# A selective scan with routed ternary experts: u\*B of 14 turns made by ScalarE and turned back by TensorE, products in place, ring of six

## The chip, the cores and the metric

One Trainium2 chip, one core. The time is the device time of one execution in microseconds (us), on the one core that runs. The engines work side by side, each with its own program in order, and meet in semaphores: TensorE (PE, with its weight loads PEld), VectorE (DVE), ScalarE (ACT), GpSimd (POOL), and SyncE (SP), which here only issues transfers.

## What is computed

Two layers on x of shape (2, 1024, 256). The scan is where the change lies; the second layer (each token goes through the weights of one of 32 masked experts) is untouched, except that its masks are brought in during the scan.

```
A = -exp(A_log);  x_dbl = x @ W_xproj.T;  delta, Bmat, Cmat = split(x_dbl, (64, 16, 16))
delta = softplus(delta @ W_dt.T + b_dt)
deltaA = exp(delta[..., None] * A)
BX = delta[..., None] * Bmat[:, :, None, :] * x[..., None]
for each time step:  h = dA * h + bx;  y = einsum('bdn,bn->bd', h, c)
y = y + D * x
```

u below is delta\*x, so that BX is u\*B.

## The kernel before, in words

Channels lie on the 128 partitions and time (L = 1024) along the free axis. There are 2 batches x 2 halves of the 256 channels = 4 groups, and 16 states n in each: 64 turns, k = 16 group + n. A turn k is:
- the decay exp(delta\*A) of 128x1024, made by ScalarE (`decay`, L562) one turn ahead
- u\*B of 128x1024. In 44 turns TensorE spreads the row of B over the partitions into PSUM (`b_rows`, L1011, two matmuls) and VectorE multiplies it by u in place (`scan`, L783). In 20 turns (states 2, 5, 8, 11, 14) SyncE brings the row of B from memory (`load_b`), and GpSimd multiplies (`bx`, L392); there ScalarE writes the decay into the PSUM buffer that no b row needs
- the scan over time on VectorE (L788), which writes h into one of four buffers
- h\*C on GpSimd (`product`, L400) into one of four more, with the row of C brought by SyncE (`load_c`)
- the sum over n on TensorE (`sums`, L1046: two matmuls with the identity, each run as two), three turns later. In states 4 to 11 `skip_and_residual` (L1035, L1037) adds D\*x and x.

The order of each engine is written out by hand in loops over k. On TensorE iteration k is: the b row of k+1 (after scan k-1), the sums of k-3, skip and residual, `prepare`, then one mask's four transposes (L1027, turns 20 to 51). `prepare` makes z of a half of delta (`delta_in`, L977; k = 1, 4, 11, 13, 15, 17) and the projection for batch 1 (`project`, L971; k = 7, 9). On ScalarE iteration k is: decay k+1, the copy of a finished delta (L513), the copy of the mask's transposes out of PSUM (`mask_out`, L550), then the soft part (`soft_part`, four ACTIVATE of 512 columns, L502 to L507) or the projection's copy (`low_out`, L491) of that iteration. All of these go through one PSUM bank, `w_ps`. VectorE finishes delta and u (`delta_u`, L756 and L758) after turns 2, 5, 12, 14, 16, 18, and converts the projection to bf16 parts after turns 8, 10, 11, 13 (L744, L748), with GpSimd in between.

The tile `xs_sb` holds h and the products in this phase, `xn` holds b rows for GpSimd, `rows` holds delta and u, `cst` the identity, `mask_sb` the masks and, late in the scan, b rows too (`b_buffer`).

## Time and profile before

| | us |
|---|---|
| median of 3 runs | 345.85 (345.0 to 347.11) |
| the profiled execution | 345.58 |
| its span in the trace | 343.7 |
| VectorE busy in the span | 297.3 (86%) |
| GpSimd busy | 271.7 (79%) |
| TensorE busy (matmul) | 251.1 (73%) |
| ScalarE busy | 159.3 (46%) |
| turns 0 to 15, start to start | 31.06 to 89.65 |
| turns 16 to 31 | 89.65 to 141.82 |
| turns 32 to 47 | 141.82 to 190.72 |
| turns 48 to 63, with the last product | 190.72 to 244.28 |

The page and the trace come from one execution, taken by the hardware profiler. A row of the timeline gives the start, the length, the engine, the line, the operation with out<-in and the count of instructions merged in it; the bracket behind it, where there is one, is the time the engine stood idle before it and who released it. PEclk is the granted clock of TensorE as a share of its full 2.4 GHz. A length is longer than the distance to the next start where neighbours overlap.

### The profile page before, as it was taken

What the parts mean: (1) busy time and instruction counts of PE and PEld (TensorE: products, weight loads), DVE (VectorE), ACT (ScalarE), POOL (GpSimd) and SP (SyncE); (2) the same over time, 40 slices, a digit from 0 to 9 for tenths busy, and PEclk for the clock granted to TensorE, in tenths of its full rate; (3) what the DMA queues carried; (4) which work ended last, traced back from release to release, by engine and by line L of the source; (5) the groups of instructions that cost most, each with busy time, mean ns of one, the idle gap of its engine ahead of it and who ended that gap; (6) DMA issues with size and microseconds to landing.
All of it is one profiled execution on the core that took longest, in us unless ns stands there. A gap on an engine that the chain in (4) does not pass through costs nothing.

```text
span 343.7 us, 3843 instructions
## 1 busy us (share of the span) xinstructions
PE 251.1 (73%) x1183; PEld 144.1 (42%) x1184; DVE 297.3 (86%) x369; ACT 159.3 (46%) x216; POOL 271.7 (79%) x153
## 2 busy tenths in 40 slices
PE   0676498994968998979899798797970006999740
PEld 0422144441324654435565344453550003899640
DVE  1999999999999999999999997999989896656650
ACT  1375755447468565556445743333265501444210
POOL 0473988999888999999999959999937770377772
PEclk9995599997889999989999989898995555999885
DMA  7425799999998799988999773762001557898400
GB/s 243 132 75 185 251 297 300 359 376 317 315 373 273 265 331 311 301 307 296 330 314 317 259 237 106 259 219 97 2 1 52 196 212 260 286 291 270 155 2 0
DMA packets 36355, 78.80 MB, mean 229 GB/s; under 512 B 5027, under 2 KB 15789, under 8 KB 36336
## 3 DMA queue, kind: packets, MB, share of 16 engines
q1 hardware_dynamic: 23744, 63.15, 55.9%
q10 hardware_dynamic: 9776, 9.09, 8.2%
q0 software_dynamic: 2816, 6.32, 4.9%
q8 instruction: 10, 0.16, 0.2%
q14 instruction: 9, 0.07, 0.1%
HBM read 63.55 MB, written 17.09 MB: 235 GB/s over the span
## 4 chain that ended last, share of the span: by engine, by line
DVE 41%; PE 20%; issue 15%; DMA 9%; POOL 7%; ACT 6%; ACTq 0%; another core or an unknown queue 0%; SPq 0%; POOLq 0%; DVEq 0%
DVE xs_sb L788 16%; PE bank L1046 11%; DVE bank L783 9%; DMA xs_sb<-sorted_tokens 4%; PE bank L1011 2%; PE bank L1198 2%; POOL out_dram L457 2%; DMA x_sb<-in_L_attn_x_dram 2%; DMA out_dram<-cb,to_token 2%; POOL sorted_tokens L447 2%; ACT dA L562 2%; DVE st L817 2%; POOL xs_sb L400 1%; DVE xn L717 1%; POOL mask_sb L392 1%
## 5 line engine op out<-in xcount | busy, mean ns | idle before, releaser
L400 POOL TENSOR_TENSOR xs_sb<-xs_sb,cb 128x1024 f32<-128x1024 f32 x63 | 147.6, 2363 | 8.0 <-DVE xs_sb L788 5.3
L1046 PE MATMUL bank<-xs_sb,cst 128*128 128x512 f32 x256 | 130.8, 639 | 1.1 <-ACT xn L567 1.1
L788 DVE TENSOR_TENSOR_SCAN xs_sb<-dA,bank 128x1024 f32<-128x1024 f32 x44 | 100.6, 2286 | 1.5
L1046 PEld LDWEIGHTS bank<-xs_sb,cst 128*128 128x128 f32 x256 | 51.0, 205 | 47.5 <-issue 38.4
L783 DVE TENSOR_TENSOR bank<-bank,rows 128x1024 f32<-128x1024 f32 x44 | 53.3, 1210 | 0.1
L1011 PE MATMUL bank<-bc,pick 96*128 96x512 bf16 x88 | 30.3, 433 | 31.0 <-DVE xs_sb L788 31.0
L562 ACT ACTIVATE dA<-rows,a_neg 128x1024 f32<-128x1024 f32 x44 | 49.5, 1139 | 0.9 <-DVE rows L756 0.5
L457 POOL DMA_INDIRECT out_dram<-cb,to_token x32 | 31.8, 993 | 22.2 <-DVE cb L934 15.4
L392 POOL TENSOR_TENSOR xn<-xn,rows 128x1024 f32<-128x1024 f32 x16 | 37.6, 2352 | 5.4 <-DMA xn<-bc_rows 5.2
L788 DVE TENSOR_TENSOR_SCAN xs_sb<-bank,xn 128x1024 f32<-128x1024 f32 x16 | 36.3, 2271 | 0.3 <-ACT bank L562 0.2
L562 ACT ACTIVATE bank<-rows,a_neg 128x1024 f32<-128x1024 f32 x20 | 22.3, 1114 | 27.5 <-DVE xs_sb L788 27.5
L550 ACT ACTIVATE wT<-bank 128x512 f16<-128x512 bf16 x32 | 19.1, 597 | 34.3 <-PE bank L1027 33.9
L671 ACT ACTIVATE xn<-bank 128x1024 f16<-128x1024 f16 x16 | 16.3, 1024 | 38.4 <-PE bank L1181 38.4
L1198 PE MATMUL bank<-wT,xn 128*128 x256 | 32.3, 283 | 0.4 <-ACT xn L671 0.4
L1198 PEld LDWEIGHTS bank<-wT,xn 128*128 128x128 f16 x256 | 25.3, 101 | 4.2 <-issue 0.9
L1011 PEld LDWEIGHTS bank<-bc,pick 96*128 96x128 bf16 x88 | 6.8, 106 | 43.6 <-DVE xs_sb L788 39.7
L447 POOL DMA_INDIRECT sorted_tokens<-rows,pos x16 | 15.8, 986 | 4.9 <-issue 4.3
L1035 PEld LDWEIGHTS bank<-xnT,diag_d 128*128 128x128 f32 x64 | 12.2, 191 | 15.6 <-issue 15.6
L926 DVE TENSOR_TENSOR cb<-bank,scale_bc 128x512 f32<-128x512 f32 x16 | 11.0, 687 | 7.7 <-PE bank L1198 7.7
L934 DVE SCALAR_TENSOR_TENSOR cb<-cb,xs_sb 128x256 f32<-128x256 f32 x32 | 14.2, 483 | 2.0 <-DVE to_token L929 0.5
L1027 PEld LDWEIGHTS bank<-ident_bf,mask_sb 128*128 128x128 bf16 x128 | 10.1, 105 | 7.9 <-issue 7.7
L1163 PE MATMUL bank<-cst,cb 64*1 64x64 f32 x2 | 0.4, 285 | 17.5 <-DVE cb L906 17.5
(142 smaller groups left out, 335.7 us busy)
## 6 DMA issues: line engine op xcount, KB each, us to landing
cb<-bc_rows SPq DMA_DIRECT2D x63, 512.0 KB, 5.4
sorted_tokens<-wT SPq DMA_DIRECT2D x32, 257.0 KB, 10.7
xn<-bc_rows SPq DMA_DIRECT2D x16, 512.0 KB, 6.7
mask_sb<-_L_ffn_expert_masks_dram ACTq DMA_DIRECT2D x32, 256.0 KB, 5.8
xs_sb<-sorted_tokens SPq DMA_DIRECT2D x7, 1028.0 KB, 8.2
x_sb<-in_L_attn_x_dram SPq DMA_DIRECT2D x4, 512.0 KB, 7.7
mask_sb<-bc_rows SPq DMA_DIRECT2D x4, 512.0 KB, 5.7
xs_sb<-sorted_tokens SPq DMA_DIRECT2D x2, 514.0 KB, 4.3
```

Of the source, the lines that this page charges most:

```text
L392: pool.tensor_tensor(b_buffer(k), b_buffer(k), u[:, dh, b * L:(b + 1) * L], ALU.mult).then_inc(s_gbx, 1)
L400: pool.tensor_tensor(prod[:, j, :], h[:, j, :], cb[:, j, :], ALU.mult).then_inc(s_prod, 1)
L447: pool.indirect_dma_start(xs, bass.IndirectOffsetOnAxis(ap=pos[:, t:t + 1], axis=0), rows[:, t, :], None).then_inc(s_scat, 16)
L457: pool.indirect_dma_start(out_v, bass.IndirectOffsetOnAxis(ap=to_token[:, 2 * f + blk:2 * f + blk + 1], axis=0), y_sb[:, f, blk, :], None, ...
L550: act.activation(wT[:, e, :, :].rearrange("p h o -> p (h o)"), mask_ps, ACT.Copy).then_inc(s_wt, 1)
L562: act.activation(to, delta[:, dh, b * L:(b + 1) * L], ACT.Exp, scale=a_neg[:, dh, n:n + 1]).then_inc(s_da, 1)
L671: act.activation(xsT_tiles[:, j, :, 0::2, :], bank[:, j, :].bitcast(fp16).rearrange("p (a s t) -> p a s t", s=2, t=M), ACT.Copy).then_inc( ...
L783: dve.tensor_tensor(bx, bx, u[:, dh, b * L:(b + 1) * L], ALU.mult).then_inc(s_bx, 1)
L788: dve.tensor_tensor_scan(h[:, j, :], decays, bx, 0.0, ALU.mult, ALU.add).then_inc(s_scan, 1)
L1011: mm = pe.matmul(b_ps[k % 2][:, c * HC:(c + 1) * HC], pick[:, n:n + 1].to_broadcast([96, P]), bc3[:, cols], start=True, stop=True)
L1046: mm = pe.matmul(yacc[:, c * HC:(c + 1) * HC], ident, prod[:, j, c * HC:(c + 1) * HC], start=first, stop=last, skip_group_check=True)
L1198: mm = pe.matmul(bank[:, 2 + f, blk * D:(blk + 1) * D], xsT[:, f % 2, blk, part, odd * M:odd * M + P], wT[:, bass.ds(experts[tile], 1), pa ...
```

## The change

- ScalarE makes u\*B of 14 turns (states 6, 8, 10, 12, 14 of group 0, states 3, 7, 11 of the others), two turns ahead. Since B varies along time and u along channels and time, it works on u with time on the partitions: TensorE turns u of the group (`turn_u`, in eight pieces over iterations 2, 3, 12, 14, 19, 20, 44, 45) and B (`turn_b`, iterations 0 and 10), ScalarE copies both out (`u_T_out`, `b_T_out`), and `act_bx` multiplies eight blocks of 128x128 by a column of B each. TensorE turns the eight blocks back into the PSUM buffer in which a b row would stand (`turn_bx`); VectorE scans from there without a multiply.
- GpSimd has 16 turns instead of 20 (states 1, 5, 9, 13), VectorE 34 instead of 44.
- A mask leaves PSUM one iteration later on ScalarE (k - 1 in place of k).
- h\*C is written over h, and the ring of h is six buffers deep: the scan of k waits for the sum of k-6, no more for the product of k-4. The room left holds u\*B turned and a b row of its own.
- The b row of the first GpSimd turn is asked for ahead of the second c row.

```diff
-POOL_STATES = (2, 5, 8, 11, 14)
+HELD = 6
+POOL_STATES = (1, 5, 9, 13)
+ACT_STATES = ((6, 8, 10, 12, 14), (3, 7, 11), (3, 7, 11), (3, 7, 11))
...
+        BT_AT = {0: 0, 10: 1}
+        UT_AT = {2: (0, 0), 3: (0, 1), 12: (1, 0), 14: (1, 1), 19: (2, 0), 20: (2, 1), 44: (3, 0), 45: (3, 1)}
...
-                if k >= masks_done:
-                    sp.wait_ge(s_mps, E - 2 + 2 * (i % 2))
+                if in_masks(i):
+                    sp.wait_ge(s_mps, E - 2)
...
-                pool.tensor_tensor(prod[:, j, :], h[:, j, :], cb[:, j, :], ALU.mult).then_inc(s_prod, 1)
+                here = h[:, k % HELD, :]
+                pool.tensor_tensor(here, here, cb[:, j, :], ALU.mult).then_inc(s_prod, 1)
...
+            def act_bx(k):
+                i, g, n = of_act[k], k // N, k % N
+                act.wait_ge(s_utsb, LH * (g + 1))
+                act.wait_ge(s_btsb, g // DH + 1)
+                if i >= 1:
+                    act.wait_ge(s_bready, of_psum[act_turns[i - 1]] + 1)
+                for c in range(LB):
+                    ins = act.activation(u_b_T[:, c, :], u_T(g)[:, c, :], ACT.Copy,
+                                         scale=b_T[:, g // DH * LB + c, n:n + 1])
+                ins.then_inc(s_abx, 1)
...
-                if 0 <= k - MASK_FROM < E:
-                    mask_out(k - MASK_FROM)
+                if 0 <= k - 1 - MASK_FROM < E:
+                    mask_out(k - 1 - MASK_FROM)
+                if k in BT_AT:
+                    b_T_out(BT_AT[k])
+                if k in UT_AT:
+                    u_T_out(*UT_AT[k])
+                if k + 2 in act_turns:
+                    act_bx(k + 2)
                 if k in SOFT_AT:
                     soft_part(SOFT_AT[k], w_ps)
...
-                if k >= RING:
-                    dve.wait_ge(s_prod, k - 3)
-                dve.tensor_tensor_scan(h[:, j, :], decays, bx, 0.0, ALU.mult, ALU.add).then_inc(s_scan, 1)
+                if k >= HELD:
+                    dve.wait_ge(s_sum, k - HELD + 1)
+                dve.tensor_tensor_scan(h[:, k % HELD, :], decays, bx, 0.0, ALU.mult, ALU.add).then_inc(s_scan, 1)
...
+            def turn_bx(k):
+                i = of_act[k]
+                pe.wait_ge(s_abx, i + 1)
+                pe.wait_ge(s_scan, k - 1)
+                for c in range(LB):
+                    mm = pe.transpose(b_ps[k % 2][:, c * P:(c + 1) * P], u_b_T[:, c, :], ident)
+                mm.then_inc(s_bready, 1)
...
-                if k + 1 < TURNS and k + 1 not in pool_turns:
+                if k + 1 in act_turns:
+                    turn_bx(k + 1)
+                elif k + 1 < TURNS and k + 1 not in pool_turns:
                     b_rows(k + 1)
```

ScalarE before, from decay 6 to the copy of the second projection (iterations 5 to 9 of group 0; L491 is that copy, and what it waits for is in the bracket):

```order
L562 ACTIVATE dA<-rows,a_neg 128x1024 [waits scan_done] x2
L513 ACTIVATE rows<-bank 128x512 [waits u_ready]
L562 ACTIVATE bank<-rows,a_neg 128x1024 [waits scan_done]
L491 ACTIVATE xd<-bank 96x512 [waits bc3_ready,bc_rows_written,z_ready,projected]
L562 ACTIVATE dA<-rows,a_neg 128x1024 [waits scan_done]
L540 DMA mask_sb<-in_L_ffn_expert_masks_dram 128x2x256 x4
L562 ACTIVATE dA<-rows,a_neg 128x1024 [waits scan_done]
L491 ACTIVATE xd<-bank 96x512 [waits bc3_ready,bc_rows_written,z_ready,projected]
```

The same stretch of ScalarE in the changed kernel (L585 is the decay, L603 `act_bx`, L512 the projection's copy):

```order
L585 ACTIVATE dA<-rows,a_neg 128x1024 [waits scan_done] x2
L534 ACTIVATE rows<-bank 128x512 [waits u_ready]
L603 ACTIVATE xs_sb<-xn,b_T 128x128 [waits b_ready,b_transposed_evacuated,u_transposed_evacuated]
L603 ACTIVATE xs_sb<-xn,b_T 128x128 x7
L585 ACTIVATE dA<-rows,a_neg 128x1024 [waits scan_done]
L512 ACTIVATE xd<-bank 96x512 [waits bc3_ready,bc_rows_written,z_ready,projected]
L585 ACTIVATE bank<-rows,a_neg 128x1024 [waits scan_done]
L561 DMA mask_sb<-in_L_ffn_expert_masks_dram 128x2x256 x4
L603 ACTIVATE xs_sb<-xn,b_T 128x128 [waits b_ready,b_transposed_evacuated,u_transposed_evacuated]
L603 ACTIVATE xs_sb<-xn,b_T 128x128 x7
L585 ACTIVATE dA<-rows,a_neg 128x1024 [waits scan_done]
L512 ACTIVATE xd<-bank 96x512 [waits bc3_ready,bc_rows_written,z_ready,projected]
```

Two blocks of eight pieces have come in, each a decay ahead of a copy that waits for TensorE's projection.

TensorE before, iterations 7 and 8 and the start of 9 (L1046 sums, L1035 and L1037 skip and residual, L971 the projection, L1011 a b row):

```order
L1046 MATMUL bank<-xs_sb,cst 128x512 [waits product_ready]
L1046 MATMUL bank<-xs_sb,cst 128x512
L1035 MATMUL bank<-xnT,diag_d 128x128
L1037 MATMUL bank<-cst,x_sb 128x128
L971 MATMUL bank<-xnT,wxT 96x512 [waits xnT_ready,xd_ready,abs_ready]
L971 MATMUL bank<-xnT,wxT 96x512
L1011 MATMUL bank<-bc,pick 128x512 [waits scan_done]
```

TensorE in the changed kernel, the same iterations (L1093 is `turn_bx`, L1127 the sums, L1116 and L1118 skip and residual, L1020 the projection):

```order
L1093 MATMUL bank<-cst,xs_sb 128x128 [waits scan_done,transposed_bx_ready]
L1093 MATMUL bank<-cst,xs_sb 128x128 x7
L1127 MATMUL bank<-xs_sb,cst 128x512 [waits product_ready]
L1127 MATMUL bank<-xs_sb,cst 128x512
L1116 MATMUL bank<-xnT,diag_d 128x128
L1118 MATMUL bank<-cst,x_sb 128x128
L1020 MATMUL bank<-xnT,wxT 96x512 [waits xd_ready,xnT_ready,u_transposed_evacuated,abs_ready]
L1020 MATMUL bank<-xnT,wxT 96x512
L1127 MATMUL bank<-xs_sb,cst 128x512 [waits product_ready]
L1127 MATMUL bank<-xs_sb,cst 128x512
L1116 MATMUL bank<-xnT,diag_d 128x128
L1118 MATMUL bank<-cst,x_sb 128x128
```

Iteration 7, which began with the sums, now begins with eight transposes that wait for ScalarE's u\*B of turn 8, and the projection stands behind them. The before list has the b row of turn 9 (its turn 9 was VectorE's, now it is GpSimd's).

## Rows read from the trace of the kernel before

**Rows 1.** Busy us and instructions per engine in two stretches, clock, DMA share, GB/s

```profile
48.40:89.70 41.30, 34.80 (x101) 16.16 (x101) 40.71 (x30) 21.33 (x27) 37.91 (x18) 0.92 1.05 345
141.80:190.70 48.90, 45.01 (x214) 25.61 (x214) 48.52 (x28) 26.84 (x33) 48.64 (x21) 0.97 0.90 308
```

**Rows 2.** Timeline of VectorE, group 2: start, us, engine, line, operation

```profile
145.27 1.21 DVE L783 TENSOR_TENSOR bank<-bank,rows 128x1024 f32<-128x1024 f32 x1
146.51 2.29 DVE L788 TENSOR_TENSOR_SCAN xs_sb<-dA,bank 128x1024 f32<-128x1024 f32 x1
148.71 2.27 DVE L788 TENSOR_TENSOR_SCAN xs_sb<-bank,xn 128x1024 f32<-128x1024 f32 x1
150.90 1.21 DVE L783 TENSOR_TENSOR bank<-bank,rows 128x1024 f32<-128x1024 f32 x1
```

**Rows 3.** Timeline of GpSimd, group 2: three products, then one u\*B

```profile
146.67 6.96 POOL L400 TENSOR_TENSOR xs_sb<-xs_sb,cb 128x1024 f32<-128x1024 f32 x3
153.59 2.35 POOL L392 TENSOR_TENSOR xn<-xn,rows 128x1024 f32<-128x1024 f32 x1
```

**Rows 4.** Waits from 60 to 236 us: total us, times, longest

```profile
DVE xs_sb L788 <- POOL mask_sb L392: 2.7, 2, 2.0
```

**Rows 5.** Timeline of ScalarE: two 128-column casts, four 256-column pieces

```profile
235.79 0.29 ACT L610 ACTIVATE ident<-cst 128x128 f16<-128x128 f32 x1
235.99 0.29 ACT L611 ACTIVATE tri_bf<-cst 128x128 bf16<-128x128 f32 x1
...
254.18 2.06 ACT L620 ACTIVATE xn<-rows,shift,rstd 128x256 f32<-128x256 f32 x4
```

**Rows 6.** Timeline of TensorE: four transposes to a mask, one whole iteration to the next

```profile
120.80 0.60 PE L1018 MATMUL bank<-cst,w_nat 128*128 128x128 f32 x4
121.24 0.39 PE L1027 MATMUL bank<-ident_bf,mask_sb 128*128 128x128 bf16 x4
...
157.98 0.60 PE L1011 MATMUL bank<-bc,pick 96*128 96x512 bf16 x2
158.41 1.88 PE L1046 MATMUL bank<-xs_sb,cst 128*128 128x512 f32 x4
160.13 0.38 PE L1035 MATMUL bank<-xnT,diag_d 128*128 128x128 f32 x2
...
160.80 0.38 PE L1011 MATMUL bank<-bc,pick 96*128 96x512 bf16 x1
```

**Rows 7.** Timeline of ScalarE, group 0: a soft part to the next decays, decay 5

```profile
35.70 0.67 ACT L502 ACTIVATE wT<-bank,bdt 128x512 f32<-128x512 f32 x1
...
38.18 2.17 ACT L562 ACTIVATE dA<-rows,a_neg 128x1024 f32<-128x1024 f32 x2
...
45.05 1.12 ACT L562 ACTIVATE bank<-rows,a_neg 128x1024 f32<-128x1024 f32 x1 [2.86 <-DVE xs_sb L788]
...
59.88 1.15 ACT L562 ACTIVATE dA<-rows,a_neg 128x1024 f32<-128x1024 f32 x1 [0.45 <-issue]
```

**Rows 8.** Timeline of VectorE, group 0: delta and u to the next multiply; turn 16

```profile
50.55 0.67 DVE L756 SCALAR_TENSOR_TENSOR bank<-wT,bank 128x512 f32<-128x512 f32 x1
...
51.87 1.22 DVE L783 TENSOR_TENSOR bank<-bank,rows 128x1024 f32<-128x1024 f32 x1
...
89.65 1.21 DVE L783 TENSOR_TENSOR bank<-bank,rows 128x1024 f32<-128x1024 f32 x1
```

**Rows 9.** Timeline of TensorE behind two idle times

```profile
148.86 0.60 PE L1011 MATMUL bank<-bc,pick 96*128 96x512 bf16 x2 [2.35 <-DVE xs_sb L788]
149.30 3.08 PE L1046 MATMUL bank<-xs_sb,cst 128*128 128x512 f32 x4
...
218.03 1.00 PE L1011 MATMUL bank<-bc,pick 96*128 96x512 bf16 x2 [1.96 <-DVE xs_sb L788]
218.83 3.22 PE L1046 MATMUL bank<-xs_sb,cst 128*128 128x512 f32 x4
```

**Rows 10.** Window behind the first of them, columns as in Rows 1

```profile
150.00:153.00 3.00, 3.00 (x8) 1.07 (x7) 2.96 (x3) 0.58 (x1) 3.00 (x2) 0.50 0.68 264
```

More of the change, by code:

```diff
@@ L105, in selective_scan_then_routed_ternary_ffn @@
         flat = "p a l -> p (a l)"
-        before = prod[:, :, :].rearrange(flat)
+        before = h_and_prod[:, 4 * L:8 * L]
         wx_nat = before[0:96, 1024:1024 + D]
@@ L199, in selective_scan_then_routed_ternary_ffn @@
         s_bload = [sem(f"b_loaded{j}") for j in range(2)]
+        s_btps = sem("b_transposed")
+        s_btsb = sem("b_transposed_evacuated")
+        s_utps = sem("u_transposed")
+        s_utsb = sem("u_transposed_evacuated")
+        s_abx = sem("transposed_bx_ready")
         s_gbx = sem("bx_ready_from_gpsimd")
@@ L986, in _, with turned_b, turned_u @@
                 delta_in(m, bank[:, m, :])
+            def turned_b(k):
+                return sum(1 for at in BT_AT if at < k)
+            def turned_u(k):
+                return sum(1 for at in UT_AT if at < k)
             def prepare(k):
@@ L1085, in _ @@
                 if k >= LAG:
-                    sums(k - LAG, (k - LAG) % RING, first=(n == LAG), last=(n == LAG - 1))
+                    sums(k - LAG, (k - LAG) % HELD, first=(n == LAG), last=(n == LAG - 1))
                 if RING <= n < RING + LB:
@@ L1091, in _ @@
                 prepare(k)
+                if k in BT_AT:
+                    pe.wait_ge(s_xnsb, 2 * DH * LH)
+                    if k:
+                        pe.wait_ge(s_low, B * LH)
+                    turn_b(BT_AT[k])
+                if k in UT_AT:
+                    pe.wait_ge(s_btsb, turned_b(k))
+                    if turned_u(k):
+                        pe.wait_ge(s_utsb, turned_u(k))
+                    pe.wait_ge(s_abs, 2 + sum(1 for at in SOFT_AT if at < k))
+                    if k > MASK_FROM:
+                        pe.wait_ge(s_wt, k - MASK_FROM)
+                    turn_u(*UT_AT[k])
                 if k == ROUTER_AT:
@@ L1129, in turn_x1 @@
                 mm.then_inc(s_yps, 1)
-            sums(TURNS - 3, (TURNS - 3) % RING)
+            sums(TURNS - 3, (TURNS - 3) % HELD)
             pe.wait_ge(s_scan, TURNS)
@@ L1137, in _ @@
             turn_x1(3)
-            sums(TURNS - 2, (TURNS - 2) % RING)
-            sums(TURNS - 1, (TURNS - 1) % RING, last=True, apart=True)
+            sums(TURNS - 2, (TURNS - 2) % HELD)
+            sums(TURNS - 1, (TURNS - 1) % HELD, last=True, apart=True)
             for c in range(LH):
```

75 lines of the change are left out of this document (54 added, 21 removed).

## The prediction

> **What bounds the kernel now.** I read the busy times by stretch first, then the timeline of VectorE, then those of the others around it, and last the waits. In the windows [rows 1], turns 32 to 47 (the third group, 48.9 us) have VectorE busy for 48.5 us and GpSimd for 48.6: two engines are full at once. TensorE is busy 45.0, and ScalarE only 26.8. In turns 5 to 15 of group 0 (41.3 us) VectorE is busy 40.7, GpSimd 37.9, ScalarE 21.3. So VectorE sets the pace throughout, GpSimd beside it from group 1 on.
>
> The timeline of VectorE gives the price of a turn from start to start [rows 2]: multiply to scan 145.27 to 146.51 = 1.24, scan to next 146.51 to 148.71 = 2.20, so 3.44 for a turn whose u\*B it makes (M turn) and 2.2 for a turn whose u\*B GpSimd makes (148.71 to 150.90). GpSimd's pieces cost (153.59 - 146.67) / 3 = 2.31 each [rows 3]. Sixteen turns cost VectorE 11 x 3.44 + 5 x 2.2 = 48.8, GpSimd 21 x 2.31 = 48.5. One more wait stands on this path: GpSimd's b row for a buffer in the mask tile comes late, and VectorE loses 2.7 us in group 3 [rows 4].
>
> **What the change takes away.** VectorE multiplies in 34 turns instead of 44: 10 x 1.24 = 12.4 us, of which 4 x 1.24 = 5.0 fall in group 0 and 2 x 1.24 in each later group (7.4). GpSimd loses 4 u\*B, 9.2 us; a group of it is then 20 x 2.31 = 46.2, VectorE's 9 x 3.44 + 7 x 2.2 = 46.4. Both go down together, so groups 1 to 3 can return 7.4 us. The b row of turn 53 is asked for three turns ahead of GpSimd's use now and only two loads go to the mask tile: I take the 2.7 us as returned as well. Four loads of 512 KB fewer, and one moved ahead of the second c row, touch nothing that waits. Product in place and the ring of six cost nothing: scan k now waits for sum k-6, which TensorE does three turns ahead. Masks out a turn late spare ScalarE waits that cost nothing, since it is half idle [rows 1].
>
> **What it adds, in the later groups.** On ScalarE a turn of its own costs eight pieces of 128 columns. The nearest rows are the plain 128-column casts, 0.20 from start to start (below), and 256-column pieces with two pointer operands, (2.06 - 0.59) / 3 = 0.49 (above) [rows 5]. The decays show what one pointer adds, some 0.09: 0.29 a piece, and 2.4 us for the eight with the last one's tail. Both ends: 1.7 and 4.0. On TensorE a turn adds eight transposes; four of the same shape take 121.24 - 120.80 = 0.44, so 0.88, in place of a b row's 0.43 [rows 6]. An iteration of TensorE with b row, sums, skip and mask takes 160.80 - 157.98 = 2.82, of which 0.43 for the row, 1.72 for the sums, 0.67 for the rest. Four turns (two with b rows, one GpSimd's, one ScalarE's) are then 2.82 + 2.39 + 2.82 + 3.27 = 11.3 against VectorE's 2 x 3.44 + 2 x 2.2 = 11.3 and GpSimd's 5 x 2.31 = 11.55. That is tight only where skip and masks meet (four such quads, one of them with logits, 0.9 more). In the others TensorE has 1.8 us of slack. I charge 3.0 us of new stalls there: 0.9 for the logits quad, some 0.3 for each other tight quad, and 1 at turns 18 to 22, where ScalarE has its last soft parts, the first y copy and the bf16 moves in a row.
>
> The Trainium skill ("ScalarE: Activation LUTs", Rules for kernel authors) budgets about 0.3 us for each ACTIVATE plus 0.83 ns an element. By that the eight would be 3.2 us, and the sum below 5 x 0.85 = 4 us longer. The casts' 0.20 from start to start speaks against it, as do their durations of 0.29, all of it included.
>
> **What it adds in group 0: the step that decides.** There ScalarE also has the soft parts, (38.18 - 35.70) = 2.5 us each, and its decays, 1.06 [rows 7]. Above all the program order now ties two engines to each other. ScalarE makes u\*B of turn k+2, then must wait for TensorE's projection or z of its next iteration; but TensorE's iteration starts with the turning back of just that u\*B, ahead of sums, skip and projection. In the kernel before, those iterations (7, 9, 11, 13) started with a b row, or with nothing, and asked ScalarE for neither. I walk it from decay 5, which starts at 45.05 now [rows 7] and, as ScalarE has copies of u and B out ahead of it, at about 45.5 after:
> - ScalarE: decay 1.06, u\*B of 6 2.4, soft part 2.5, decays 6 and 7 2.1, a copy 0.55, u\*B of 8 2.4: 11.0 (56.6)
> - TensorE, iteration 7: 0.1 + 0.88 + 1.72 + 0.44 + projection 1.72 + tail 0.16 = 5.0 (61.6)
> - ScalarE: copy 0.6, decay 1.06, issue of four mask loads 0.45 [rows 7], u\*B of 10 2.4: 4.5 (66.1)
> - TensorE, iteration 9, the same 5.0, and iteration 10 (row 0.43, sums 1.72, skip 0.44, turning B 0.88): 3.5 (74.6)
> - ScalarE: B out 0.3, u\*B of 12 2.4: 2.7 (77.3)
> - TensorE, iteration 11: 0.1 + 0.88 + 1.72 + 0.44 + z 0.86 + 0.16 = 4.2 (81.5)
> - ScalarE: soft part 2.5, decay 1.06, u out 0.55, u\*B of 14 2.4: 6.5 (88.0)
> - TensorE, iteration 13, no skip: 3.7 (91.7)
> - ScalarE soft part 2.5, then VectorE delta and u (51.87 - 50.55 = 1.32 [rows 8]) and turn 15 at 3.44: 7.3 (99.0).
>
> Turn 16 starts at 99.0 instead of 89.65 [rows 8]: **+9.3 us**, although VectorE has 5.0 less to do. VectorE stands still in between (the scans of 10 and 12, the conversions after 8 and 10, deltas 4 and 5), and nothing covers it: GpSimd waits for the same scans.
>
> On top, TensorE is idle in this walk for 2.5 us before iteration 9, 2.8 before 11 and 4.4 before 13. After an idle time of 2.35 us and one of 1.96 us the profile shows the granted clock at 0.50, of its two levels 1.2 GHz, and four sums take over 3 us [rows 9, 10]; a stretch of 3 us at that level costs 1.5 to 1.7. Before, that cost nothing; now these iterations are on the path. Three times 1.6: **+4.8**.
>
> **Sum**, against the profiled execution of 345.58 (span 343.7), which is within 0.3 us of the median 345.85: +9.3 + 4.8 - 7.4 - 2.7 + 3.0 = +7.0, so 352.6 us.
>
> **Rivals.**
> - *The clock stays up, or the pieces are cheap.* Idle times of just over 2 us might miss a fall. For: at 148.86 the row itself was still fast. Without the 4.8 the time is 347.8; with pieces at 0.20 as well (5 x 0.7 less) about 344. Chance 0.26, nearly all of it within 1%.
> - *The pieces are dear*, as two pointers' 0.49 would have them: 1.6 more for each of five in group 0 (+8), and in the tight quads of the later groups TensorE waits for them: about 362. With the 0.3 us and 0.83 ns of the Trainium skill ("ScalarE: Activation LUTs", Rules) it would be 357. The copy with one pointer is nearer to a plain cast. Chance 0.15.
> - *TensorE becomes the bound in the later groups*: 11.3 us of work in 11.3, so each fall of the clock and each late piece stays. Some four losses of 1.6: 359. Against: outside skip and mask turns it has slack to catch up. Chance 0.10.
> - *Faster: ScalarE and TensorE do not hold each other in group 0.* ScalarE's own work for turns 5 to 16 is 12 decays, 5 u\*B, 4 soft parts, 8 copies: 39.4 us, so it would be through by 85, and turn 16 could start near 87, 2.6 earlier than now. With 7.4 and 2.7 returned and 1 of stalls, 334. It decides from the point where its waits for TensorE in group 0, 15 us in the walk, fall under some 3. For: VectorE alone needs less. Against: the order of the two programs, and waits of the same kind are there already. Chance 0.08.
>
> The forecast itself has 0.41. Range 344.5 to 359: from the cheap end of the first rival to the third. A measurement of this kernel tells about 1% from no change, 342.4 and 349.3. Slower 0.41 + 0.15 + 0.10 = 0.66; faster 0.09 (the last rival and the edge of the first); the same 0.25.
>
> **What would show it.** In the new timeline turn 16's multiply starts at 97 to 105 us; ScalarE waits for TensorE before the two projections' copies and soft parts 4 and 5 by 2 to 4 us each; TensorE waits for ScalarE's u\*B before iterations 9, 11 and 13, with the granted clock at 0.50 behind it; the pieces start 0.29 apart; groups 2 and 3 take 46.4 to 48 us each, and the 2.7 us at the mask buffer are gone. I am wrong if turn 16 starts before 93, or if groups 1 to 3 give back less than 7 us in all, for then a bound that I hold for slack has moved in.

## The result and the profile after

The changed kernel takes 353.91 us (median of 4 executions, 352.4 to 355.75) against 346.48 for the kernel before on the same chip: ratio 1.0225, 95% interval 1.0182 to 1.0268. It is slower by 2.2%; the whole interval lies above 1. The forecast was 352.6 with a range of 344.5 to 359. The profiled execution is the one of 352.4 us (span 350.6), so it is 6.9 us of span longer than the one of before. Two of the traces read below, of the kernels called "projection and z first" and "the same, u\*B before mask", come from slow executions, 1.6% above the fastest of their kernel, which the ratios leave out.

Reading the time by stretch, from the window view: start and end, length, busy us and instructions of TensorE, its weight loads, VectorE, ScalarE and GpSimd, then granted clock, DMA share, GB/s. The four stretches are turns 5 to 15, and groups 1, 2 and 3 up to VectorE's last product.

```profile
47.80:100.50 52.70, 40.84 (x155) 21.45 (x154) 34.25 (x25) 34.49 (x70) 37.88 (x18) 0.97 1.01 306
100.50:153.50 53.00, 45.04 (x213) 25.64 (x213) 49.15 (x30) 39.84 (x70) 45.23 (x20) 1.00 0.77 240
153.50:204.70 51.20, 45.88 (x232) 27.36 (x231) 46.62 (x26) 34.64 (x59) 46.83 (x21) 0.97 0.85 286
204.70:251.80 47.10, 43.42 (x184) 24.54 (x183) 46.16 (x26) 27.18 (x48) 45.74 (x21) 1.00 0.53 190
```

Against [rows 1]: in turns 5 to 15 VectorE's work fell from 40.7 us to 34.3, but the stretch grew from 41.3 to 52.7, so VectorE, which was full, now stands still a third of the time, and GpSimd's 37.9 are the same work spread wider. In group 2 VectorE's work fell by 1.9 and the stretch grew by 2.3; no engine fills it now. Only in group 3 does the length follow VectorE's work again.

The same in positions (start of a turn's first VectorE instruction, us):

| turn | before | after | shift | gained or lost since the turn above |
|---|---|---|---|---|
| 16 | 89.65 | 100.53 | +10.9 | +10.9 |
| 32 | 141.82 | 153.54 | +11.7 | +0.8 |
| 48 | 190.72 | 204.72 | +14.0 | +2.3 |
| last product | 243.00 | 251.85 | +8.9 | -5.2 |
| end of span | 343.7 | 350.6 | +6.9 | -1.9 |

Where VectorE stands still in group 0, from its timeline (start, us, line, operation; in brackets the idle time ahead of it and what ended it). The row of turn 16 is the last; before, it stood in [rows 8].

```profile
67.00 2.29 DVE L838 TENSOR_TENSOR_SCAN xs_sb<-dA,bank 128x1024 f32<-128x1024 f32 x1 [1.91 <-PE bank L1093]
71.50 0.56 DVE L793 CAST bc<-xd 32x512 bf16<-32x512 f32 x1 [2.21 <-ACT xd L512]
77.88 2.29 DVE L838 TENSOR_TENSOR_SCAN xs_sb<-dA,bank 128x1024 f32<-128x1024 f32 x1 [1.78 <-PE bank L1093]
83.69 0.70 DVE L805 SCALAR_TENSOR_TENSOR bank<-wT,bank 128x512 f32<-128x512 f32 x1 [3.52 <-ACT bank L528]
...
95.74 0.69 DVE L805 SCALAR_TENSOR_TENSOR bank<-wT,bank 128x512 f32<-128x512 f32 x1 [4.73 <-ACT bank L528]
...
100.53 1.21 DVE L833 TENSOR_TENSOR bank<-bank,rows 128x1024 f32<-128x1024 f32 x1
```

L1093 is TensorE turning u\*B back, L512 ScalarE's copy of the projection, L528 the last step of a soft part. The releasers alternate between TensorE and ScalarE, as two engines that hold each other would show. Their own timelines have the other half: ScalarE (first fence) waits for TensorE's projection (L1020) and z (L1026), TensorE (second fence) for ScalarE's u\*B (L603).

```profile
61.11 0.59 ACT L512 ACTIVATE xd<-bank 96x512 f32<-96x512 f32 x1 [4.02 <-PE bank L1020]
...
74.09 0.28 ACT L589 ACTIVATE b_T<-bank 128x128 f32<-128x128 f32 x1 [1.58 <-PE bank L1077]
74.26 2.43 ACT L603 ACTIVATE xs_sb<-xn,b_T 128x128 f32<-128x128 f32 x8
...
81.09 0.69 ACT L523 ACTIVATE wT<-bank,bdt 128x512 f32<-128x512 f32 x1 [3.36 <-PE bank L1026]
...
93.14 0.69 ACT L523 ACTIVATE wT<-bank,bdt 128x512 f32<-128x512 f32 x1 [4.08 <-PE bank L1026]
```

```profile
65.87 1.09 PE L1093 MATMUL bank<-cst,xs_sb 128*128 128x128 f32 x8 [2.63 <-ACT xs_sb L603]
66.80 1.88 PE L1127 MATMUL bank<-xs_sb,cst 128*128 128x512 f32 x4
...
76.75 1.09 PE L1093 MATMUL bank<-cst,xs_sb 128*128 128x128 f32 x8 [2.69 <-ACT xs_sb L603]
77.68 1.88 PE L1127 MATMUL bank<-xs_sb,cst 128*128 128x512 f32 x4
...
87.59 1.10 PE L1093 MATMUL bank<-cst,xs_sb 128*128 128x128 f32 x8 [4.18 <-ACT xs_sb L603]
88.52 3.38 PE L1127 MATMUL bank<-xs_sb,cst 128*128 128x512 f32 x4
```

The four sums take 1.88 us behind idle times of 2.63 and 2.69, and 3.38 behind that of 4.18. The windows (length, busy TensorE, granted clock, DMA share, GB/s) show why: the clock fell to 0.50, its lower level of 1.2 GHz, once in this stretch, and TensorE's idle time of 4.18 us ends just ahead of it.

```profile
76.00:78.00 2.00, 1.25 (x9) 1.00 0.91 311
...
88.00:90.00 2.00, 2.00 (x10) 0.69 1.04 304
90.00:92.00 2.00, 2.00 (x4) 0.50 0.97 220
```

And VectorE's waits from turn 16 on (total us, times, longest); of [rows 4] nothing is left.

```profile
DVE bank L833 <- PE bank L1070: 5.8, 6, 1.6
DVE xs_sb L838 <- ACT dA L585: 1.0, 1, 1.0
DVE xs_sb L838 <- ACT bank L585: 0.8, 1, 0.8
DVE xs_sb L838 <- PE bank L1093: 0.5, 1, 0.5
```

They are 8.1 us in nine places: 0.77, 1.63 and 0.96 before turns 21, 24 and 27 (3.4 in group 1); 1.58, 0.38, 0.54, 0.90 and 0.75 before turns 36, 40, 43, 44 and 46 (4.2 in group 2); 0.58 before turn 52.

### The profile page after: what moved, and what is told of

Same layout as the page of the kernel before. It is cut to its first block, busy times and chain, and to the rows that moved or that the text cites. A ratio compares the mean times of both kernels' runs of the same rounds, so it can differ in the third digit from the quotient of the medians.

```text
span 350.6 us, 4272 instructions
## 1 busy us (share of the span) xinstructions
PE 255.9 (73%) x1324; PEld 153.9 (44%) x1324; DVE 282.2 (80%) x359; ACT 194.8 (56%) x338; POOL 263.6 (75%) x149
## 4 chain that ended last, share of the span: by engine, by line
PE 27%; DVE 23%; ACT 17%; issue 16%; DMA 8%; POOL 6%; ACTq 1%; SPq 0%; POOLq 0%; DVEq 0%
PE bank L1127 13%; ACT xs_sb L603 7%; DVE xs_sb L838 5%; DVE bank L833 5%; POOL out_dram L478 4%; DMA out_dram<-cb,to_token 4%; PE bank L1093 3%; DMA x_sb<-in_L_attn_x_dram 2%; POOL sorted_tokens L468 2%; PE bank L1070 2%; PE bank L1020 2%; DVE st L866 1%; ACT dA L585 1%; PE bank L1108 1%; PE bank L1012 1%
## 5 line engine op out<-in xcount | busy, mean ns | idle before, releaser
L1127 PE MATMUL bank<-xs_sb,cst 128*128 128x512 f32 x256 | 125.6, 615 | 1.1 <-ACT xn L610 1.1
L838 DVE TENSOR_TENSOR_SCAN xs_sb<-dA,bank 128x1024 f32<-128x1024 f32 x48 | 109.1, 2283 | 7.3 <-PE bank L1093 5.2
L1127 PEld LDWEIGHTS bank<-xs_sb,cst 128*128 128x128 f32 x256 | 47.6, 196 | 41.3 <-issue 35.0
L585 ACT ACTIVATE dA<-rows,a_neg 128x1024 f32<-128x1024 f32 x48 | 54.3, 1139 | 0.6 <-DVE rows L805 0.5
L833 DVE TENSOR_TENSOR bank<-bank,rows 128x1024 f32<-128x1024 f32 x34 | 41.3, 1216 | 6.1 <-PE bank L1070 5.8
L603 ACT ACTIVATE xs_sb<-xn,b_T 128x128 f32<-128x128 f32 x112 | 34.1, 389 | 0.7 <-issue 0.7
L1070 PE MATMUL bank<-bc,pick 96*128 96x512 bf16 x68 | 22.6, 416 | 9.1 <-DVE xs_sb L838 9.0
L1093 PE MATMUL bank<-cst,xs_sb 128*128 128x128 f32 x112 | 15.2, 279 | 15.3 <-ACT xs_sb L603 15.3
L585 ACT ACTIVATE bank<-rows,a_neg 128x1024 f32<-128x1024 f32 x16 | 17.8, 1114 | 10.8 <-DVE xs_sb L838 10.8
L413 POOL TENSOR_TENSOR xs_sb<-xs_sb,rows 128x1024 f32<-128x1024 f32 x8 | 18.8, 2355 | 3.3 <-DVE rows L807 3.3
L1093 PEld LDWEIGHTS bank<-cst,xs_sb 128*128 128x128 f32 x112 | 12.1, 142 | 18.5 <-ACT xs_sb L603 18.5
L1116 PEld LDWEIGHTS bank<-xnT,diag_d 128*128 128x128 f32 x64 | 12.2, 190 | 15.3 <-issue 15.3
L838 DVE TENSOR_TENSOR_SCAN xs_sb<-bank,xs_sb 128x1024 f32<-128x1024 f32 x8 | 18.2, 2270 | 0.6 <-PE bank L1127 0.6
L1108 PE MATMUL bank<-ident_bf,mask_sb 128*128 128x128 bf16 x128 | 12.4, 220 | 6.1 <-ACT wT L571 4.2
```

Source lines behind the costliest of these rows:

```text
L585: act.activation(to, delta[:, dh, b * L:(b + 1) * L], ACT.Exp, scale=a_neg[:, dh, n:n + 1]).then_inc(s_da, 1)
L603: ins = act.activation(u_b_T[:, c, :], u_T(g)[:, c, :], ACT.Copy, scale=b_T[:, g // DH * LB + c, n:n + 1])
L833: dve.tensor_tensor(bx, bx, u[:, dh, b * L:(b + 1) * L], ALU.mult).then_inc(s_bx, 1)
L838: dve.tensor_tensor_scan(h[:, k % HELD, :], decays, bx, 0.0, ALU.mult, ALU.add).then_inc(s_scan, 1)
L1070: mm = pe.matmul(b_ps[k % 2][:, c * HC:(c + 1) * HC], pick[:, n:n + 1].to_broadcast([96, P]), bc3[:, cols], start=True, stop=True)
L1093: mm = pe.transpose(b_ps[k % 2][:, c * P:(c + 1) * P], u_b_T[:, c, :], ident)
```

## The experiments

The experiments ran on four chips. On two of them the kernel before takes 346 us, on the others 357 and 358; each ratio is to the kernel before on the same chip in the same batch. Positions inside the loop do not depend on the chip (below), so they are compared across all of them. The table gives the starts of turns 16, 32 and 48 and the end of the last scan.

| kernel | turn 16 | turn 32 | turn 48 | last scan ends | ratio to before, 95% |
|---|---|---|---|---|---|
| before | 89.65 | 141.82 | 190.72 | 242.9 | 1 |
| after | 100.53 | 153.54 | 204.72 | 251.8 | 1.0225 (1.0182 to 1.0268) |
| after, again | 102.56 | 155.57 | 206.77 | 253.8 | 1.0219 (1.0172 to 1.0266) |
| no u\*B in group 0 | 91.17 | 145.14 | 194.69 | 241.7 | 0.9957 (0.9906 to 1.0008) |
| projection and z first | 92.38 | 145.41 | 194.97 | 242.0 | 0.9889 (0.9846 to 0.9932) |
| one piece | 95.82 | 148.13 | 196.39 | 242.8 | 0.9975 (0.9939 to 1.0011) |
| masks in time | 102.59 | 166.86 | 230.35 | 279.1 | 1.0998 (1.0930 to 1.1066) |
| before, masks late | 88.82 | 140.29 | 189.09 | 240.9 | 0.9997 (0.9963 to 1.0030) |
| no u\*B on ScalarE | 90.81 | 144.71 | 194.78 | 244.9 | 1.0024 (0.9997 to 1.0052) |
| mask before y | 101.41 | 155.38 | 203.81 | 250.5 | one execution, 355.22 to 346.07 |
| no skip (no u\*B in group 0) | 90.57 | 143.00 | 191.43 | 238.5 | one execution, 339.61 to 346.07 |
| TensorE filled | 99.54 | 153.56 | 204.78 | 251.8 | 1.0204 (1.0149 to 1.0259) |
| first and four | 89.10 | 142.89 | 191.31 | 237.7 | 0.9860 (0.9823 to 0.9897) |
| the same, u\*B before mask | 91.75 | 144.19 | 193.16 | 241.3 | 0.9844 (0.9772 to 0.9915) |

**The theory** is the prediction's: group 0 is lost because the order of two programs ties ScalarE and TensorE to each other. Its rivals: ScalarE's own work is too much there (the pieces), or the falls of the clock are what costs.

### Group 0: without its u\*B on ScalarE

```diff
-ACT_STATES = ((6, 8, 10, 12, 14), (3, 7, 11), (3, 7, 11), (3, 7, 11))
+ACT_STATES = ((), (3, 7, 11), (3, 7, 11), (3, 7, 11))
```

> The changed kernel with no ScalarE turn in group 0 (its five are VectorE's again; u of group 0 is still turned). Theory A, the order ties ScalarE and TensorE together in group 0: VectorE's own work sets group 0 (12 x 3.44 + 4 x 2.2 + 9.2 for deltas and conversions = 59.3 us from 30.3), turn 16 starts at 90 to 91 instead of 100.5, and the time falls by some 10 us to 344. Theory B, the loss lies in what group 0 does for the turned copies of u and B and in the in-place ring: turn 16 stays above 97 and the time above 351.

Turn 16 starts at 91.17, 9.4 earlier, and all of it reaches the end of the loop (241.7 against 251.8). The part for group 0 alone costs the changed kernel its whole loss; the ratio, 0.9957 (0.9906 to 1.0008), cannot be told from that of the kernel before. Of the 1.5 us by which turn 16 still lies behind [rows 8], 1.2 are one multiply more in this stretch: GpSimd made u\*B of turns 8, 11 and 14 there, and makes that of 9 and 13 now.

ScalarE waits for TensorE here as long as in the changed kernel: for the two projections, z and the turned B 18.4 us from 48 us to turn 16, against 17.3 there. Those waits cost nothing as long as TensorE does not wait for ScalarE in turn. In this kernel it does not in that stretch; in the changed one it waits five times (total us, times, longest):

```profile
PE bank L1093 <- ACT xs_sb L603: 11.9, 5, 4.2
```

### Group 0: the same work in another order

```diff
+                if k in PROJECT_AT or (k in SOFT_AT and k > 1):
+                    prepare(k)
                 if k + 1 in act_turns:
                     turn_bx(k + 1)
...
-                prepare(k)
+                if k == 1:
+                    prepare(k)
```

> The changed kernel, but TensorE's projection or z of an iteration stands ahead of the transposes that wait for ScalarE's u*B. Nothing else moves. Theory A (the order ties the two engines): the waits of ScalarE for the projections and soft parts 4 and 5 (15.6 us in the profile after) fall under 7, turn 16 starts at 91 to 95, and the time is 345 to 349. Theory C (ScalarE's own work is too much in group 0, 12 decays, 40 pieces and 4 soft parts): turn 16 stays at 98 to 101, since those are as long as before, and the time moves by less than 2 us.

Nothing is taken away here, ScalarE has all five turns; only TensorE makes projection and z ahead of the turning back. Turn 16 starts at 92.38, 8.15 earlier, and the time falls below that of the kernel before. ScalarE's waits for the projections and for z, 15.5 us in the changed kernel, are gone; it waits 8.4 us for the turned B and u instead. VectorE's waits up to turn 16 were 18.1 us in nine places (nearly all of the difference between its 34.3 us of work and 52.7); three are left, one of 1.22 at 51.66 and these:

```profile
84.72 2.29 DVE L838 TENSOR_TENSOR_SCAN xs_sb<-dA,bank 128x1024 f32<-128x1024 f32 x1 [3.40 <-PE bank L1093]
...
92.38 1.23 DVE L833 TENSOR_TENSOR bank<-bank,rows 128x1024 f32<-128x1024 f32 x1 [0.60 <-PE bank L1070]
```

That separates the theory from the first rival: the amount of work is the same and the time is gone, so it was the order. The gain in time is larger than the trace shows: by the ratio the kernel is 1.1% (4 us) faster than the one before, and in the trace the last scan ends only 0.9 us earlier (242.0 against 242.9). Where the rest lies is open.

### Group 0: cheaper pieces

```diff
-                for c in range(LB):
-                    ins = act.activation(u_b_T[:, c, :], u_T(g)[:, c, :], ACT.Copy,
-                                         scale=b_T[:, g // DH * LB + c, n:n + 1])
+                ins = act.activation(u_b_T[:, :, :], u_T(g)[:, :, :], ACT.Copy,
+                                     scale=b_T[:, g // DH * LB, n:n + 1])
```

> The changed kernel, but ScalarE makes u*B turned in one ACTIVATE of 1024 columns with one column of B for all eight blocks, so that the values of h in 14 turns are others than the reference's; the transposes stay. It costs 1.14 instead of 2.43 us. Theory A: each of the five in group 0 is on the path, 5 x 1.3 = 6.5, turn 16 starts near 94, and the time is 346 to 348.5. Theory D (TensorE alone holds VectorE there, ScalarE's pieces are covered): less than 2 us of it is seen.

The line groups of ScalarE (count | busy, mean ns) give the price of both, the changed kernel in the first fence:

```profile
L603 ACT ACTIVATE xs_sb<-xn,b_T 128x128 f32<-128x128 f32 x112 | 34.1, 389 | 0.7 <-issue 0.7
```

```profile
L602 ACT ACTIVATE xs_sb<-xn,b_T 128x1024 f32<-128x1024 f32 x14 | 15.9, 1139 | 0.7 <-issue 0.7
```

Eight pieces take 2.43 from first to last, one takes 1.14: 1.29 less a turn. Turn 16 starts at 95.82, 4.7 earlier, which is 3.6 of the five savings: most of them were on the path. This trace has one fall of the clock there, as the first of the changed kernel, so the difference is not the clock's. The size of ScalarE's work counts only because it stands in a ring of waits; the ring itself remains (VectorE still waits 2.21, 2.88 and 4.10 us there).

### Group 0: the clock alone

```diff
                 i = of_act[k]
+                if k in FILL:
+                    pe.wait_ge(s_scan, k - 1)
+                    for t in range(FILL[k]):
+                        pe.transpose(b_ps[k % 2][:, t % LB * P:(t % LB + 1) * P], ident, ident)
                 pe.wait_ge(s_abx, i + 1)
...
+FILL = {10: 22, 12: 22, 14: 36}
```

> The changed kernel with TensorE kept busy while it waits for u*B of turns 10, 12 and 14: 22, 22 and 36 transposes of the identity into the bank that the real ones then overwrite, 0.11 us each, so 2.4, 2.4 and 3.9 us in idle times of 2.6, 2.7 and 4.2. Mine (a fall of the clock there costs 1.6 to 2 us each, and how many there are differs from execution to execution): the granted clock stays at 1.00 from 58 to 100 us, turn 16 starts at 98.5 to 99.2 (100.5 and 102.6 in the two traces of the changed kernel, with one fall and with two), ratio to the kernel before 1.012 to 1.018 instead of 1.022. Rival (the four slow sums are hidden behind ScalarE's soft part, and the clock is worth nothing there): turn 16 at 100.3 or later, ratio 1.020 or more.

TensorE's timeline at turn 14: the filler, the real transposes, the sums. The granted clock is 1.00 in every window from 54 to 100 us.

```profile
83.89 4.09 PE L1094 MATMUL bank<-cst 128*128 128x128 f32 x36
88.24 1.09 PE L1098 MATMUL bank<-cst,xs_sb 128*128 128x128 f32 x8 [0.25 <-ACT xs_sb L604]
89.17 1.88 PE L1132 MATMUL bank<-xs_sb,cst 128*128 128x512 f32 x4
```

From the scan of turn 14 to turn 16 it takes 99.54 - 89.37 = 10.17 us, in the changed kernel 100.53 - 88.72 = 11.81. One fall on this path costs 1.6 us, the price that the prediction gave it. Turn 16 itself is at 99.54, later than the 98.5 to 99.2 expected, since this execution was 0.6 behind from turn 5 on. The ratio does not tell the two theories apart: 1.0204 with an interval of 1.1%; it lies above the 1.012 to 1.018 expected. So the price of a fall rests on the two traces.

### The changed kernel once more

> The changed kernel itself, beside the kernel before, on a second chip, where the runs of the kernel before were some 10 us longer than on the first. Mine: the loop over the turns takes what it took (turn 16 starts at 100.5, the last scan ends at 251.8), and the whole 10 us stand behind it, so the ratio to the kernel before is 1.020 to 1.025. Rival: the longer part behind the loop hides some of the loss, ratio under 1.015.

The kernel before takes 346 us on this chip too, so nothing was learned here of one where it takes longer. The trace is worth more. From the scan of turn 8 to that of turn 12 it takes 19.74 us, as in the first, from there to turn 16 25.47 instead of 22.65. TensorE, behind the same idle time that had cost nothing:

```profile
75.96 1.10 PE L1093 MATMUL bank<-cst,xs_sb 128*128 128x128 f32 x8 [2.70 <-ACT xs_sb L603]
76.89 3.32 PE L1127 MATMUL bank<-xs_sb,cst 128*128 128x512 f32 x4
```

The clock fell behind 2.70 us of waiting here, and not behind 2.69 in the first execution. How many falls there are is a matter of the execution: one after turn 5 of group 0 in the first (352.4 us), two in this one (355.4), the second at a price of 2.8 us, since it reached into the next iterations.

### The late masks

In the changed kernel masks leave PSUM in the next iteration. Back to their own iteration, behind the copies of u and B and ahead of u\*B:

```diff
-                if 0 <= k - 1 - MASK_FROM < E:
-                    mask_out(k - 1 - MASK_FROM)
                 if k in BT_AT:
                     b_T_out(BT_AT[k])
                 if k in UT_AT:
                     u_T_out(*UT_AT[k])
+                if 0 <= k - MASK_FROM < E:
+                    mask_out(k - MASK_FROM)
```

> The changed kernel, but a mask leaves PSUM in its own iteration again (the copies of turned u and B stand ahead of it, so that no two waits close a ring). In the profile after, TensorE's mask transposes of iteration 34 wait 1.7 us for the copy of the mask before, which now stands behind the copy of y, and VectorE then waits 1.6 us for the b row. Theory E (the late mask copies make this wait): the waits at turns 36 and 52 go, time 350.5 to 352.5, 1.5 to 3 less. Theory F (TensorE is simply full in groups 1 and 2): within 0.7 of the changed kernel, or slower, since ScalarE's u*B then waits for each mask.

The ratio is 1.0998, far slower than either theory put it; only the second had the direction. Groups 1 and 2 take 64.3 and 63.5 us. Waits from 100 to 260 us:

```profile
ACT wT L571 <- PE bank L1108: 50.1, 29, 5.7
...
PE bank L1093 <- ACT xs_sb L603: 21.4, 8, 3.5
```

TensorE makes a mask at the end of an iteration; ScalarE waits for it before it makes u\*B, and TensorE's next iteration begins with that u\*B: the same ring as in group 0, closed at each u\*B turn of groups 1 and 2. The prediction was right that late masks cost nothing, and its reason ("spare ScalarE waits that cost nothing") was not: without the delay those waits close a ring as soon as u\*B is made on ScalarE. That they do nothing by themselves is shown by the kernel before with the same one-iteration delay:

```diff
-                if 0 <= k - MASK_FROM < E:
-                    mask_out(k - MASK_FROM)
+                if 0 <= k - 1 - MASK_FROM < E:
+                    mask_out(k - 1 - MASK_FROM)
```

> The kernel before, with only the mask copies of ScalarE moved one iteration later. Mine: nothing, ratio 1.000 within 0.5%, turn 16 at 89.7 and the last scan ending at 243: ScalarE's waits for masks (34 us) shrink to some 20, but no one waited for ScalarE. Rival: a late mask copy holds TensorE's next mask and so VectorE's b row, as at turn 36 of the changed kernel: 1.6 us for each of the places where a y copy stands in between, the last scan ending at 245 to 248, ratio 1.005 to 1.013.

Ratio 0.9997, and 2 us less of loop in one trace, which the times do not confirm.

### What u\*B on ScalarE is worth in the later groups

```diff
+ACT_STATES = ((), (), (), ())
```

> The changed kernel with no u*B on ScalarE at all: VectorE makes 48 of them, GpSimd 16; ring of six, products in place and late masks stay. Mine (the stalls of the later groups come with ScalarE's turns): the groups take VectorE's work, 1.24 more than before in each: turn 16 at 92, then 53.4, 50.3 and 47.2 to turn 63, the last scan ending at 246.5; that is 5 less than the changed kernel and 5 more than with the group 0 part alone undone; ratio to the kernel before 1.005 to 1.012. Rival (the stalls come with the ring, the fewer GpSimd turns or the late masks): the waits for the b row of 1.6, 1.6, 0.9 and 0.7 stay, the last scan ends at 252 or later, ratio 1.02 or more.

The ring of six, the products in place and the fewer turns of GpSimd stay, and VectorE waits 1.2 us in all. Set beside the kernel that differs from it by nine turns on ScalarE, no u\*B in group 0 (first fence this kernel from 44 us on, second the other from 92 us on, the rows up to the end of the loop):

```profile
DVE bank L805 <- ACT bank L528: 1.0, 2, 0.8
DVE xs_sb L838 <- ACT bank L585: 0.2, 1, 0.2
```

```profile
DVE bank L833 <- PE bank L1070: 4.2, 5, 1.6
DVE xs_sb L838 <- ACT dA L585: 1.0, 1, 1.0
DVE xs_sb L838 <- ACT bank L585: 0.9, 1, 0.9
DVE bank L805 <- ACT bank L528: 0.8, 1, 0.8
DVE xs_sb L838 <- PE bank L1093: 0.5, 1, 0.5
```

Groups 1, 2 and 3 (to turn 63) take 53.9, 50.1 and 46.6 us without, 54.0, 49.6 and 43.5 with. Three multiplies less are 3.7 us of VectorE in each: group 3 gives back 3.1 of them, group 2 0.5, group 1 nothing. The new stalls come with ScalarE's u\*B, not with the ring, and the theory that named the ring or the masks falls. The sizes were off: the last scan ends at 244.9 (246.5 expected), and the ratio 1.0024 is below the 1.005 to 1.012 expected.

### Is it TensorE that is full there?

```diff
-                if RING <= n < RING + LB:
-                    skip_and_residual(g, n - RING)
```

on top of the kernel without u\*B in group 0.

> The changed kernel without u*B on ScalarE in group 0 and without the skip and residual products of TensorE (so y lacks both terms, and what is computed from it is other data; the order of the work behind it stays). Mine (in groups 1 and 2 VectorE's b rows come late since TensorE has as much work as VectorE there): of the waits at turns 24 (1.64), 40 (0.38), 46 (0.90) and 48 (0.74) three are gone, and the last scan ends at 238.5 to 240 instead of 241.7. Rival (ScalarE is late with u*B and masks, TensorE only passes it on): the waits stay within 0.3 of what they are, end at 241.2 or later.

The waits before turns 27, 40, 44 and 46 (the last two are those that the expectation puts at 46 and 48) are gone or at 0.2; groups 1 and 2 take 52.4 and 48.4 instead of 54.0 and 49.6; the last scan ends at 238.5 instead of 241.7. This trace also has a fall of the clock at turn 33 and behind it a wait of 1.50 before turn 36 that the kernel with the skip does not have, so the 3.2 us understate what was freed. By the single waits 3.6 of the 7.4 us are gone. So TensorE's load is the larger part of the waits before turns 27 to 46. It is not all of the wait before turn 24, which only went from 1.64 to 1.19: in the iterations ahead of it TensorE waits for ScalarE's copy of u (1.71 us) and its u\*B (1.08). The waits before turns 18, 21 and 52 (0.76, 0.87 and 0.57) stay as they were.

### The wait before turn 36

I first read the 1.6 us before turn 36 as a late mask: ScalarE's mask copy stands behind its y copy, and TensorE waits 1.69 us for it. The test puts the mask copy ahead:

```diff
+                if 0 <= k - 1 - MASK_FROM < E:
+                    mask_out(k - 1 - MASK_FROM)
                 if k >= N and k % N == LAG - 1:
                     y_out(k // N - 1)
-                if 0 <= k - 1 - MASK_FROM < E:
-                    mask_out(k - 1 - MASK_FROM)
```

> The changed kernel with ScalarE's late mask copy ahead of its y copy. Mine (the mask copy that stands behind the y copy holds TensorE at turns 34 and 50, and with it the b row of turn 36): TensorE's waits of 1.69 before the mask transposes fall under 0.9, VectorE's wait of 1.6 before turn 36 is gone, group 2 takes 49.6 instead of 51.2. Rival (that wait comes from a fall of the clock ahead of it): the wait at turn 36 stays at 0.5 to 1.6 where the clock fell, and is absent where it did not, whatever stands first.

The wait is gone and group 2 takes 48.4, which looks like a hit. For the wait before turn 36 it is not one. TensorE at turn 33 in the changed kernel, then in this one:

```profile
155.44 0.38 PE L1108 MATMUL bank<-ident_bf,mask_sb 128*128 128x128 bf16 x4 [0.81 <-ACT wT L571]
157.13 1.04 PE L1070 MATMUL bank<-bc,pick 96*128 96x512 bf16 x2 [1.31 <-DVE xs_sb L838]
157.95 3.12 PE L1127 MATMUL bank<-xs_sb,cst 128*128 128x512 f32 x4
```

```profile
157.28 0.38 PE L1108 MATMUL bank<-ident_bf,mask_sb 128*128 128x128 bf16 x4 [0.81 <-ACT wT L571]
158.97 0.61 PE L1070 MATMUL bank<-bc,pick 96*128 96x512 bf16 x2 [1.31 <-DVE xs_sb L838]
159.41 1.88 PE L1127 MATMUL bank<-xs_sb,cst 128*128 128x512 f32 x4
```

The same idle times, and the clock fell in one and not in the other. The kernels without u\*B in group 0 and with projection and z first have the old order, TensorE's wait of 1.70 for the mask, no fall, and no wait of VectorE there. Of the kernels with the old order of the copies, the wait before turn 36 is there in the four traces in which the clock fell at turn 33 (after, after again, no skip, TensorE filled) and absent in the four in which it stayed up (no u\*B in group 0, projection and z first, one piece, no u\*B on ScalarE). The rival on record was right for turn 36: the fall is the cause, and the late mask alone costs nothing there. Whether the new order would cover such a fall is left open. The last kernel below had a fall there and no wait, but it has u\*B ahead of the mask as well.

The new order is still worth something elsewhere. Without a fall at turn 33 group 2 takes 49.6 us in the old order (no u\*B in group 0, projection and z first), and 48.4 here and in the next kernel, and the waits before turns 40, 43 and 52 (0.38, 0.55 and 0.58) are gone in both. VectorE's waits for b rows from turn 16 on, six in the changed kernel, are three here (before turns 24, 44 and 46), and none is left for u\*B turned back:

```profile
DVE bank L833 <- PE bank L1070: 3.3, 3, 1.6
```

### A version that beats both

Projection and z first, turn 14 back to VectorE (`(6, 8, 10, 12)` for group 0), the mask copy ahead of the y copy.

> The changed kernel with three edits: TensorE makes projection and z ahead of turning u*B back, turn 14 goes back to VectorE, and the mask copy stands ahead of the y copy on ScalarE. Mine: turn 16 at 90.2 (92.4 with the first edit alone, less its wait of 3.4 before turn 14, plus 1.24), groups 1 and 2 as there (53.0 and 49.6), the last scan ending at 239.8, ratio to the kernel before 0.980 to 0.986. Rival (what holds group 0 is ScalarE's own work): turn 16 stays at 92 or later, ratio 0.989 or more.

340.94 us, ratio 0.9860 (0.9823 to 0.9897): 1.4% faster than the kernel before, 3.5% than the changed one in the same batch (0.9860 / 1.0219). Turn 16 starts at 89.10, 1.1 earlier than expected, group 1 takes 53.8 (53.0 expected), group 2 48.4 (49.6), and the last scan ends at 237.7 (239.8). A further edit, u\*B ahead of the mask copy from turn 21 on, was tried on it:

```diff
+                if k > MASK_FROM and k + 2 in act_turns:
+                    act_bx(k + 2)
                 if 0 <= k - 1 - MASK_FROM < E:
                     mask_out(k - 1 - MASK_FROM)
```

> The version of 0.986 (projection and z first, four turns of ScalarE in group 0, mask copy ahead of y copy) with u*B ahead of the mask copy on ScalarE in groups 1 to 3. Mine: TensorE's waits for u*B of 0.64, 0.62 and 0.42 go, 0.6 to 1.3 us of the loop come back, ratio 0.982 to 0.986. Rival: the mask copy, now 2.4 us later, makes TensorE wait before its next mask transposes, and the b row behind them: 0.5 to 2 us in each of six or seven places, ratio 0.990 to 1.02.

0.9844 (0.9772 to 0.9915) cannot be told from 0.9860. In its trace TensorE no longer waits for u\*B of turn 23, but 0.94 us for the mask copy behind it, and VectorE's wait before turn 24 is still there (1.79). On this one trace it reads like a trade and not a gain.

## Why the prediction came out

The total was right, and part of it because errors cancelled. By its own terms, against the profiled execution:

| term | predicted | measured |
|---|---|---|
| walk of group 0 | +9.3 | +9.3 (10.9 less one fall) |
| clock, group 0 | +4.8 | +1.6 in this execution, 4.4 in the second |
| multiplies returned, groups 1 to 3 | -7.4 | -7.4 (34 instead of 44 in the page) |
| mask buffer wait | -2.7 | -2.7 |
| new stalls in the later groups | +3.0 | +8.1 |
| behind the loop | 0 | -1.9 |
| sum | +7.0 | +7.0, against 6.9 measured |

- **The walk held at every station.** Copy of the projection at 61.11 (61.6 in the walk), B out at 74.09 (74.6), soft part 4 at 81.09 (81.5), soft part 5 at 93.14 (91.7 plus one fall). The waits named for ScalarE and TensorE are those of the trace, and changing TensorE's order alone gives 8.15 us back. It is shown that this ring of waits is the cause.
- **The price of a piece held**: 2.43 for eight, 0.29 from start to start, against 2.4. The rival of dear pieces (362 or 357) was out with this row. The Trainium skill ("ScalarE: Activation LUTs", Rules for kernel authors) has about 0.3 us for each ACTIVATE and 0.83 ns an element: 3.2 us for the eight, where the trace has 2.43, and 1.15 for the one piece of 1024 columns, where it has 1.14. The same page (What ACT_TABLE_LOAD costs) has the missing part: 186 ns and 0.833 ns an element, 93 more for a pointer operand, and 93 by which two in a row overlap. That is 0.29 from start to start for a piece, and the trace agrees.
- **The clock was sized wrong in number, right in price.** Three falls of 1.6 were charged; there was one after turn 5 of group 0, and two in a second execution, where they cost 4.4 together. The filled kernel has 1.6 for one. The step that failed is "Three times 1.6", a fall for each of the idle times of 2.5, 2.8 and 4.4 us: [rows 9] showed two falls behind shorter idle times, and I read a rule out of two cases.
- **The new stalls in the later groups were 8.1, not 3.0.** Of these, 1.6 is a fall of the clock at turn 33 that the term did not have. The other 6.5 come with ScalarE's u\*B: 4.2 are waits for TensorE's b rows, 0.5 for u\*B turned back, 1.8 for ScalarE's decays. The sum 11.3 against 11.3 was in the prediction, in four quads, and was priced at 0.3 to 0.9 each. The failing step is that price, with the slack taken for sure outside those quads: 1.3 us of the waits (before turns 46 and 52) stand behind iterations in which TensorE was to have slack. By the waits that went with the skip products, 3.6 of the 6.5 are TensorE's fullness. Ahead of turn 24 the trace has what is not caught up in a stretch without slack: a wait of 1.26 for ScalarE's copy of the turned u, u\*B 0.63 late, router products of 1.3 us. The wait before turn 52 went with the mask copy first; for the wait before turn 21 and most of that before turn 24, some 2 us, no cause is shown. So of the 10.1 us that groups 1 to 3 should give back, 2.0 arrived (7.1 net in the prediction). The prediction had named this as the sign that a bound held for slack had moved in, and it had: in group 1, ScalarE's three turns give back nothing. That its total came out rests on luck here: the clock charged 3.2 too much and the stretch behind the loop was 1.9 shorter, the new stalls 5.1 too little.
- **The mask buffer's 2.7 us** came back: no wait for GpSimd's b row is left, and group 3 is 5.2 us shorter, where 2.5 of multiplies and 2.7 less 0.6 of a new wait make 4.6.
- **Behind the loop** -1.9 is no part of the change: from the last scan's end to the end of the span it took 98.8 and 99.8 us in the two traces of the changed kernel, 100.8 before, and 99.2 to 102.9 in the six others where the kernel before takes 346 us.

## What to carry to other kernels

When work moves to a half idle engine, its busy share says nothing yet: write down for both engines what stands ahead of the new work and what its user does first with it. If the user begins its step with the moved result, and the maker's next step begins with what that user makes last, each pays for the other in every round; here putting projection and z ahead of the moved result was worth 8 us of 354, with not one instruction less. And a stretch in which a second engine's sum equals the first's has no room for what comes late: where the estimate here was 3 us of stalls, 6.5 came, besides a fall of the clock.
